# Two waits for eight products of a group, four for a chunk turn, in the edge loop of a graph layer kernel

## The reference

```python
xn = layernorm(x)
gathered = (xn @ W_neighbor)[src] * edge_weight[:, None]
x = x + xn @ W_self + segment_sum(gathered, dst, 6250) + bias + mix(xn)   # mix: linear attention, 8 heads
x = x + ffn(layernorm(x))    # 8 experts, the best 2 of each token
```

## Time and profile before

| | |
|---|---|
| median of 3 runs (lowest to highest) | 3308.7 us (3300.01 to 3310.05) |
| profiled execution | 3332.17 us |
| its span, first to last instruction | 3330.3 us |
| granted TensorE clock, mean | 0.841 |
| PE busy | 2487.6 us, 75% |
| DVE busy | 1335.1 us, 40% |
| ACT busy | 972.5 us, 29% |
| POOL busy | 1502.3 us, 45% |
| DMA, mean | 82 GB/s |

### The profile page before, as it was taken

How to read it: one execution, slowest core, us unless ns; L and a number is a source line. 1 busy time by engine, 2 the same in 40 slices (tenths; PEclk the granted TensorE clock), 3 DMA queues, 4 the chain that set the end, 5 groups by cost and what they waited for, 6 DMA issues and landing times. The chain is left out here.

```text
span 3330.3 us, 60899 instructions
## 1 busy us (share of the span) xinstructions
PE 2487.6 (75%) x11706; PEld 1966.7 (59%) x11707; DVE 1335.1 (40%) x3211; ACT 972.5 (29%) x3042; POOL 1502.3 (45%) x1632
## 2 busy tenths in 40 slices
PE   5566665776666766668766776768767999999998
PEld 4344444554444544455545544545656999999997
DVE  6644444334344244443444343442566222222222
ACT  2254433313233122321222122220114333333332
POOL 3533344344444355544555455554011555545454
PEclk8777887787777887778878887788878999999999
DMA  6311122332222322224222422234580222222222
GB/s 221 126 43 57 49 63 58 90 101 61 63 65 77 113 80 77 81 81 126 85 79 82 140 73 84 80 90 127 159 314 12 35 36 36 36 36 36 36 36 32
DMA packets 163687, 272.80 MB, mean 82 GB/s; under 512 B 29868, under 2 KB 120364, under 8 KB 163308
## 3 DMA queue, kind: packets, MB, share of 16 engines
q0 software_dynamic: 76640, 186.99, 21.6%
q1 hardware_dynamic: 79392, 74.26, 7.1%
q10 hardware_dynamic: 7600, 10.96, 1.1%
HBM read 232.65 MB, written 39.45 MB: 82 GB/s over the span
## 5 line engine op out<-in xcount | busy, mean ns | idle before, releaser
L740 POOL DMA_INDIRECT big<-support_d,big x1088 | 1041.1, 957 | 1150.9 <-PE psBB L1006 716.1
L1001 PE MATMUL psBB<-big 128*128 (+1 forms) x2176 | 615.3, 438 | 136.4 <-issue 91.2
L1001 PEld LDWEIGHTS psBB<-big 128*128 128x128 f32 x2176 | 466.8, 222 | 273.6 <-issue 200.6
L910 DVE TENSOR_SCALAR R_<-big 128x196 f32 x768 | 328.2, 472 | 597.8 <-issue 291.3
L897 DVE TENSOR_SCALAR big<-big 128x128 f32 x1088 | 308.5, 353 | 422.7 <-PE psBB L1001 183.6
L1482 POOL DMA_INDIRECT out<-accs,sidx x104 | 236.6, 2275 | 291.9 <-DVE accs L1556 277.7
L1017 PE MATMUL psE<-R_,xn 128*128 128x196 f32 x696 | 212.3, 450 | 189.7 <-issue 92.4
L1017 PE MATMUL psD<-R_,xn 128*128 128x196 f32 x840 | 234.3, 422 | 157.7 <-issue 79.7
L1017 PEld LDWEIGHTS psD<-R_,xn 128*128 128x128 f32 x840 | 171.9, 238 | 193.3 <-issue 189.0
L1017 PEld LDWEIGHTS psE<-R_,xn 128*128 128x128 f32 x696 | 150.0, 252 | 223.0 <-issue 218.7
L772 ACT ACTIVATE xn<-sup,ones 128x128 f32<-128x128 f32 x420 | 141.8, 390 | 407.2 <-issue 362.6
(11 more groups left out here) (275 smaller groups left out, 2827.3 us busy)
## 6 DMA issues: line engine op xcount, KB each, us to landing
big<-support_d SPq DMA_DIRECT2D x140, 128.0 KB
big<-support_d,big POOLq DMA_INDIRECT x1088
big<-w POOLq DMA_DIRECT2D x16, 1024.0 KB, 13.0
sup_s_<-support_d SPq DMA_DIRECT2D x105, 128.0 KB
big<-xnT_d SPq DMA_DIRECT2D x98, 128.0 KB, 4.1
accs<-x ACTq DMA_DIRECT2D x7, 896.0 KB, 11.2
out<-accs SPq DMA_DIRECT2D x7, 896.0 KB, 10.7
xnT_d<-xT SPq DMA_DIRECT2D x25, 128.0 KB, 1.8
```

The costliest lines, as they stand in the source:

```text
L740: nc.gpsimd.indirect_dma_start(out=G[:, s, t, :], out_offset=None, in_=support_d, in_offset=bass.IndirectOffsetOnAxis(ap=idxs[:, s * GT + ...
L910: nc.vector.tensor_scalar(R[:, s * UNROLL + t, :].rearrange("p (h d) -> p h d", d=WIDE), places, key[:, c], wts[:, c], ALU.is_equal, ALU.m ...
L1001: nc.tensor.matmul(psBB[:, bank, 0:D], S[:, t, :], G[:, bass.ds(slot, 1), t, :].rearrange("p a d -> p (a d)"), start=(t == 0), stop=(t == ...
```

## The change

In the edge loop the waits of three engines are drawn together. A number of products or selections that each had a wait of its own now has one wait for several.

- PE, groups: the first product waits until six of the eight selections are there (a count of `n * GT + 7`, since the semaphore starts at 1), the seventh until all are; the others do not wait.
- DVE, groups: the first selection waits until four products of the group before are done, the fifth until all eight are.
- PE, chunk turns: the first product waits for two `L` and two `R`, the third for all three.
- DVE, chunk turns: the first selection waits until two products of the turn before are done, the third until all are.
- ACT, chunk turns: the first absolute difference waits for all three relus of the turn before; the first relu for one absolute difference and one product, the second for all three of each; the third does not wait.

```diff
--- before.py
+++ after.py
@@ -762,13 +762,19 @@
                     with act.Fori(pb, end) as kk:
                         for t in range(UNROLL):
                             c = chunk(act, kk, pb, f, t)
-                            act.wait_ge(l_ready[s], kk * UNROLL + t + 1)
+                            if t == 0:
+                                act.wait_ge(l_ready[s], kk * UNROLL + UNROLL)
                             nc.scalar.activation(apart[s][:, t, :], iota[:, :], ACT.Abs, bias=nlo[:, bass.ds(c, 1)],
                                                  scale=1.0).then_inc(abs_ready[s], 1)
                         for t in range(UNROLL):
-                            wait_apart(act,
-                                       (abs_ready[s], kk * UNROLL + t + 1),
-                                       (lr_used[s], kk * UNROLL + t + 1))
+                            if t == 0:
+                                wait_apart(act,
+                                           (abs_ready[s], kk * UNROLL + 1),
+                                           (lr_used[s], kk * UNROLL + 1))
+                            elif t == 1:
+                                wait_apart(act,
+                                           (abs_ready[s], kk * UNROLL + UNROLL),
+                                           (lr_used[s], kk * UNROLL + UNROLL))
                             nc.scalar.activation(L[:, s * UNROLL + t, :], apart[s][:, t, :], ACT.Relu, bias=ones[:, 0:1],
                                                  scale=-1.0).then_inc(l_ready[s], 1)
 
@@ -893,7 +899,8 @@
                         dve.wait_ge(s_ready, n * GT + 1)
                         for t in range(GT):
                             c = bass.ds(g * GT + t, 1)
-                            dve.wait_ge(s_used, n * GT + t + 1)
+                            if t % (GT // 2) == 0:
+                                dve.wait_ge(s_used, n * GT + t + GT // 2)
                             nc.vector.tensor_scalar(S[:, t, :], nodes[:, bass.ds(b * P, P)], dstf[:, c], wts[:, c],
                                                     ALU.is_equal, ALU.mult).then_inc(s_ready, 1)
                         add_sum(n + 1)
@@ -906,7 +913,10 @@
                     with dve.Fori(pb, end) as kk:
                         for t in range(UNROLL):
                             c = bass.ds(chunk(dve, kk, pb, f, t), 1)
-                            dve.wait_ge(lr_used[s], kk * UNROLL + t + 1)
+                            if t == 0:
+                                dve.wait_ge(lr_used[s], kk * UNROLL + 2)
+                            elif t == UNROLL - 1:
+                                dve.wait_ge(lr_used[s], kk * UNROLL + UNROLL)
                             nc.vector.tensor_scalar(R[:, s * UNROLL + t, :].rearrange("p (h d) -> p h d", d=WIDE),
                                                     places, key[:, c], wts[:, c],
                                                     ALU.is_equal, ALU.mult).then_inc(r_ready[s], 1)
@@ -997,7 +1007,10 @@
                         pe.wait_ge(ps_free, n + 1)
                         bank = within(pe.snap(n & 1), 0, 1)
                         for t in range(GT):
-                            pe.wait_ge(s_ready, n * GT + t + 2)
+                            if t == 0:
+                                pe.wait_ge(s_ready, n * GT + GT - 1)
+                            elif t == GT - 2:
+                                pe.wait_ge(s_ready, n * GT + GT + 1)
                             nc.tensor.matmul(psBB[:, bank, 0:D], S[:, t, :],
                                              G[:, bass.ds(slot, 1), t, :].rearrange("p a d -> p (a d)"),
                                              start=(t == 0), stop=(t == GT - 1)).then_inc(s_used, 1)
@@ -1011,9 +1024,14 @@
                     nc.tensor.matmul(mark[s], zeros[:, :], zeros[:, 0:1], start=True, stop=False)
                     with pe.Fori(pb, end) as kk:
                         for t in range(UNROLL):
-                            wait_apart(pe,
-                                       (l_ready[s], kk * UNROLL + t + 1 + UNROLL),
-                                       (r_ready[s], kk * UNROLL + t + 1))
+                            if t == 0:
+                                wait_apart(pe,
+                                           (l_ready[s], kk * UNROLL + UNROLL + 2),
+                                           (r_ready[s], kk * UNROLL + 2))
+                            elif t == UNROLL - 1:
+                                wait_apart(pe,
+                                           (l_ready[s], kk * UNROLL + 2 * UNROLL),
+                                           (r_ready[s], kk * UNROLL + UNROLL))
                             nc.tensor.matmul(part[s], L[:, s * UNROLL + t, :], R[:, s * UNROLL + t, :],
                                              start=False, stop=False).then_inc(lr_used[s], 1)
                     nc.tensor.matmul(mark[s], zeros[:, :], zeros[:, 0:1], start=False, stop=True).then_inc(summed[s], 1)
```

## The result

| | before | changed |
|---|---|---|
| median of 16 runs | 3309.4 us | 3332.5 us |
| lowest to highest | 3268.9 to 3317.3 | 3317.3 to 3362.0 |
| ratio, 95% interval | | 1.0111 (1.0083 to 1.0140) |

The change makes the kernel slower: by 1.1% by the ratio in the last row, which is not the quotient of the two medians. These lie 23 us or 0.7% apart. The forecast was 3263 us and faster. The time lies inside the range of 3205 to 3342, on the side that had 0.26.

What follows compares the result with a forecast made beforehand. The prediction took PE's own queue instructions to bound the edge loop where gathers run. It summed -72 - 21 + 47 = -46 us against the profiled 3332.2, giving 3286, or 3263 us against the median; range 3205 to 3342.

Steps and rivals of the forecast that it cites:

- the side that had 0.26: The chance given to the whole kernel coming out slower, against 0.57 for faster and 0.17 for the same.
- What bounds the kernel: Edge loop, 2216 of 3330 us: in stretches with gathers, register instructions take 0.7 us and the queue's own instructions bound.
- What goes on PE, 72 us, and on DVE and ACT, 21: Edge loop: dropped register and semaphore instructions save 72 us on PE and 21 us of its waits for DVE and ACT.
- 6/19 and 3/12 of "issue": Shares of PE's idle time waiting for no other engine taken as saved: 29 us in groups, 43 in chunk turns.
- What the coarser waits add, 47 us, at most 85: PE's later first products: 53 us in groups, 32 in chunk turns, 85 if all stays; 47 taken.
- 43 against 32 us: PE's chunk turns: 43 us saved by dropped instructions, 32 us added by starting one selection later.
- Does it stay?: Edge loop: PE starting later finds the next R and L ready, so 47 of 85 us of lateness stay.
- DVE's and ACT's later refill, nothing: Edge loop: DVE ending selections later and ACT's later first absolute difference add nothing; without cover DVE's would be 38 us.
- The slower one: First product of groups and turns: lateness outweighs dropped instructions, +77 us (3386), middle case +39 (3348); chance 0.26.
- No change: Edge loop: dropped instructions lie under running products, so 3309 us, from 3300 to 3318; chance 0.17.
- The clock's gain: Edge loop: less idle time raises PE's granted clock from 0.79 to 0.83, 73 us less, 3190 us; chance 0.13.
- What would show it: PE's waits: "issue" near 60 us at groups and 130 at turns, DVE's at groups 80 or 100, if right.

Runs made afterwards that it cites:

- e6: The kernel before, unchanged, run again with a profile beside the changed kernel; ratio 0.9985.
- e5: The whole change, run again with a profile, against the kernel before; ratio 1.0111.
- e9: Kernel before with its fine waits, plus as many increments of `passed` as the change drops instructions, on PE, DVE and ACT; ratio 1.0405.
- e10: Changed kernel with its coarse waits, plus an increment of `passed` for each dropped instruction, against the kernel before; ratio 1.0216.
- e8: Only DVE's and ACT's waits coarse, PE waiting for each selection, against the kernel before; ratio 0.9985.
- e15: Only PE's waits in chunk turns coarse, against the kernel before; ratio 0.9982.
- e16: Only DVE's waits coarse, in groups and chunk turns, against the kernel before; ratio 1.0006.
- e12: Staggered PE waits, the first product needing one selection or one L and R; DVE's group waits as in the change; against the kernel before, ratio 1.0022.
- e3: Only the groups' waits of the change, on PE and DVE, against the kernel before in a session where that took 2635 us; ratio 1.0169.
- e11: Only PE's waits in groups coarse, against the kernel before; ratio 1.0128.
- e2: Kernel before, fine waits, with as many increments of `passed` added as the change drops instructions, in a session where the kernel before took 2635 us; ratio 1.0250.
- the first pair: The first profiled executions, one of the kernel before and one of the changed kernel: 3332.2 us and 3317.3 us.
- e4: Only the chunk turns' waits of the change, on PE, DVE and ACT, against the kernel before in a session where that took 2635 us; ratio 1.0169.

## Why the prediction was wrong

The forecast was -46 us, and measured was +37 (1.11% of 3309), 83 off. Two steps of the sum failed, and the larger one is the gain: 58 of the 83 us are there, 24 in the lateness.

**What bounds the kernel.** Right as far as the loop goes: it carries the difference, and the stage behind it stayed within some 3 us (776.7 and 778.7 in e6 and e5). That the queues' own instructions matter there is shown too: adding 3168 costs 134 us (e9).

**What goes on PE, 72 us, and on DVE and ACT, 21.** This step failed first: 93 us were forecast, and 35 came back (e10 less e5, between 13 and 56). It took a share of an engine's idle time by cause, 6/19 and 3/12 of "issue", as if it could be taken off the total. With the same waits and the shorter queues (e10 to e5) "issue" fell by 60 us and the waits for ACT by 62, but those for DVE rose by 141. Nor did e8, e15, e16 or e12, each with part of the instructions gone, come out faster than the kernel before beyond its interval. That a shorter queue on one engine uncovers the next engine's is the likely reason; it is argued and not shown, since no run drops an instruction without drawing a wait together.

**What the coarser waits add, 47 us, at most 85.** Too small: 71 us (e10), inside its own ends. What each group costs was read from rows 8, a stretch in which selections follow each other every 0.254 us, while in the two groups shown, with slow instructions, they are mostly 0.7 to 2 us apart. That can't be all that was missed: the count above puts most of the added idle time outside such groups, and e3, with its instructions dropped as well, lost 1.7%, 45 us, in a calm session without a single one. The place was right: PE's waits in the groups (1.0128 or 42 us by themselves, e11). For the chunk turns the terms were 43 against 32 us, and PE's part came out even (0.9982, e15).

**Does it stay?** A little over half was taken, on the ground that PE would find R and L ready. For ACT that was so, 74.1 to 10.8 us; for R it wasn't, 91.7 to 202.6. With 85 in place of 47 the term would have been above the 71 measured.

**DVE's and ACT's later refill, nothing.** Right in a dear session (e8, e16).

**The rivals.** The slower one had the right place, the first product of a group, and in its middle case both sizes: 85 us of lateness and 46 of gain, +39, where 71, 35 and +37 were measured. "No change": the cited passage of the Trainium skill (VectorE: DVE Perf Modes, "The DRAIN you can't avoid") isn't tested here as it stands. What was added in e2 and e9 are instructions of their own in the queues, and those aren't free. The clock's gain didn't come: 0.80 before, 0.79 after in the loop. Rows 4 were read too simply for that rival: their third stretch has PE busy for 7.56 of 8 us at a granted clock of 0.63, behind one in which it was busy for 3.28 of 15.

**What would show it.** "Issue" before the products gave the sign for right in one place only, the chunk turns of the first pair: 66 to 92 us at groups and 171 to 148 at chunk turns in e6 and e5, 91 to 74 and 172 to 120 in the first pair, where 60 and 130 stood for right. The waits for DVE at groups did: "to 80 or 100" for right, measured 139.6, a rise of 90 against a fall of 88 in "issue" over all lines. The waits for R and L came to 211 us, short of the 250 named.

What stays open: how large the gain would be without coarse waits; what sets the price of lateness in groups that aren't drawn out; why some sessions have the slow instructions and others don't; and what in the chip makes a register instruction take 0.7 us. That it is in stretches with gathers is shown in rows 4 to 6; but in calm sessions the gathers run as well, at 115 GB/s.

## What to carry to other kernels

An engine's idle time by cause is not a list of savings: take one cause away and the engine arrives sooner at its next wait. Where a consumer works behind its feeder, a wait drawn together for the first item costs directly (1.0128 for PE's group waits alone). Give the first item its own wait and let later waits cover several (1.0022 instead of 1.0111 here); even so nothing was gained. Adding an instruction doesn't price its removal: 134 us for 3168 added, 35 for as many dropped. And a profile is one execution: compare it with the median of its kernel before a difference between two profiles is explained.

## What the runs showed of the hardware

The same program took 2635 or 3307 us on the same chip, in different sessions, with the other runs of a session close by. In a calm session no ALU_OP of PE's in the loop is above 42 ns (e2). In a dear one 214 of its 4339 take more than 600 ns (e6). Counted with those of DVE, ACT and SP and their other register instructions (FUSED_REGOPS, MOVE) it is 1055 in the loop of e6 and none in that of e2. In POOL's queue, which issues the gathers, no register instruction of the loop takes more than 79 ns in either. The loop is some 700 us longer with it (e9 and e2), more than anything that the change could move. How much of that the slow instructions cause isn't shown, since the loop's granted clock differs as well, 0.78 and 0.98. Coarse waits in the chunk turns were 1.7% slower in a calm session (e4), and in a dear one PE's part of them was free (e15); the three engines' waits together weren't measured there.
